# Chunked delta-rule attention on one core: another order of the same work on TensorE, VectorE, ScalarE and GpSimd

## The chip, the cores and the metric

The kernel runs as one program on one core of a Trainium2 chip. The metric is the device time of one execution in microseconds (us). Below, PE is TensorE, PEld its weight loads, DVE is VectorE, ACT is ScalarE, POOL is GpSimd, and SP is the engine whose queue issues the DMAs.

## The reference, cut to what matters

The program is a chain of blocks on x of 2 x 2048 rows by 256: an FFN, the attention, the FFN again, a binary-weight FFN, a state-space convolution, and the binary FFN again. The change lies in the attention alone, a gated delta rule with 16 heads of width 16 and chunks of 64 rows:

```python
q = l2norm((x @ Wq).reshape(Bb, Tt, H, K)) / np.sqrt(K)
k = l2norm((x @ Wk).reshape(Bb, Tt, H, K))
v = (x @ Wv).reshape(Bb, Tt, H, K)
gate = (x @ Wg).reshape(Bb, Tt, H, K)
...
P = jnp.where(strict, jnp.einsum('bhncd,bhnmd->bhncm', k_beta, k) * L, 0.0)
Ainv = jnp.eye(C, dtype=P.dtype) + P
Pk = P
for _ in range(int(np.ceil(np.log2(C))) - 1):
    Pk = Pk @ Pk
    Ainv = Ainv + Pk @ Ainv
v = Ainv @ v
k_cumdecay = Ainv @ (k_beta * jnp.exp(g)[..., None])

def step(S, inp):
    q_i, k_i, v_i, kcd_i, g_i, L_i = inp
    attn = jnp.where(tril, jnp.einsum('bhck,bhmk->bhcm', q_i, k_i) * L_i, 0.0)
    v_new = v_i - kcd_i @ S
    o_i = q_i * jnp.exp(g_i)[..., None] @ S + attn @ v_new
    ...
o = o * jax.lax.rsqrt(jnp.mean(o * o, axis=-1, keepdims=True) + 1e-05) * norm_w
o = o * jax.nn.silu(gate)
return o.reshape(Bb, Tt, D) @ Wo
```

## The kernel before, in words

The attention goes over 32 tiles of 128 rows. It works in blocks of 32 rows, so that a tile has four blocks, done in two halves of the state's recurrence. Each engine has its own instruction stream, in which one loop over 41 slots (`for n in range(-1, SLOTS)`) calls short functions; `at(f, t)` calls `f` for tile `t` where such a tile exists. An engine runs its stream strictly in order, and a `wait_ge` on a semaphore holds all that stands behind it. So the order in which the loops name the functions is the schedule, and nothing else decides it. Different functions of one slot work on different tiles:

- **Tile n.** `norm_x` (DVE, normalizes x), `turn_x` (PE, L1051, transposes it), `keep_xt` (ACT, L1252, copies it out of PSUM), `project_qk` (PE, L1060), `squares` (ACT), `sum_qk` and `guess_qk` (DVE), `root_qk` (POOL, twelve small operations of a reciprocal root), `scale_q` and `scale_k` (DVE, L1424 and L1432), `project_vg` (PE, L1070), `keep_gate` (DVE), and on POOL `spread_decays`, `strengths`, `decayed_k`, `decayed_kb`, `decayed_q`.
- **Tile n-1.** `decays`, `turn_kq`, `turn_kb` and `within` (PE; `within` is L1111, the products inside a block), the ACT copies `keep_kq`, `keep_kb`, `keep_qg`, `exp_decays`, and on DVE `keep_within` (L1442 into delta_PT) and `keep_attn` (L1442 into delta_AT).
- **Two tiles at a time, the substitution.** SP writes delta_PT to memory (L1030, four DMAs of a tile). For a pair m it then waits for both tiles' writes, reads the pair back in another layout into delta_PR (L1012, `pair_in`), waits for the end of the substitution of the pair before it, writes that pair's result out (L1017, `pair_back`), waits for it, and reads it into delta_T as 8 DMAs (L1025, four for each tile). The substitution itself (`solve`, L1468 to L1478) is 60 steps on DVE: 30 in an odd slot and 30 in the slot behind it. It starts with a memset (L1468) that waits for the pair to have landed. Every step waits for the step before it, since each uses its result. Steps 0 to 23 work on 30 to 228 columns, steps 24 to 52 on about 130 to 240, and steps 54 to 59 on 84 or fewer.
- **Tile n-5.** `apply` (PE, L1133) needs delta_T; ACT copies its result with `keep_wt` (L1327) and `keep_ut` (L1319). `spread_vk` (L1312, four copies) fills the operand of the next `apply`.
- **Tile Z = n-6, the recurrence.** For each half: `from_values` (L1146), `from_state` (L1163), ACT `keep_y`, PE `to_state` (L1180), DVE `own_heads` (L1486, into delta_Bm) and `new_state` (L1493, L1498). POOL's `fade_first`, `middle_state`, `fade_second` and ACT's `widen` stand beside it. Then `outputs` (L1195, L1200) and ACT's `keep_o`.
- **Tiles n-7 and n-8, the output.** `sum_o`, `guess_o` (DVE), `root_o` (POOL), `scale_o` (DVE), `gate_o` (POOL, L1637), `turn_o` (PE, L1211), `keep_ot` (ACT, L1371), `project_o` (PE, L1219), `add_o` (DVE, L1516, adds to the residual), `new_stats`.

PSUM bank 7 is shared: its lower half holds the turned o, and one quarter of it the state's product; its upper half holds first the turned x and then the result of `project_o`.

## Time and profile before

| | |
|---|---|
| three runs | 1584.12, 1571.48, 1567.22 us; median 1571.48 |
| profiled execution | 1571.99 us, span 1570.2 us |
| busy, share of the span | PE 77%, DVE 68%, POOL 38%, ACT 32% |
| mean granted TensorE clock | 0.856 of full speed |
| the attention's slots | from about 306 us to 1042 us of the span |

The profile page gives the busy time of each engine and a picture of the span in 40 slices. The attention is the stretch in which DMA traffic is steady at 50 to 57 GB/s, and what runs into it and out of it. Rows below come from three views: the list of waits (which operation stood idle for which other one, summed), the timeline of one engine, and the table of busy time by stretch.

### The profile page before, as it was taken

The page shows a single profiled execution, that of the slowest core. Times are in us where ns is not written, and L with a number is a line of the kernel's source. Part 1 is how long each engine was busy: PE and PEld are TensorE (multiplying, and loading weights), DVE is VectorE, ACT ScalarE, POOL GpSimd, SP SyncE. Part 2 cuts the span into 40 slices and gives each one's busy share as a digit, 9 for nine tenths or more (in the row PEclk, how much of TensorE's full clock was granted, in tenths as well). Part 3 has the DMA queues.
Part 4 walks back from the last instruction along what each step waited for, and adds up shares of the span by engine and source line. Part 5 has one row for each costly group of instructions (what it writes and reads, how often), then busy time and mean ns, then how long its engine had stood idle before and what let it go on. Part 6 is the DMA issues. An engine that isn't in the chain of part 4 may idle for free. (4 is left out here: it accounts for less than half of the span.)

```text
span 1570.2 us, 42564 instructions
## 1 busy us (share of the span) xinstructions
PE 1206.5 (77%) x17194; PEld 893.8 (57%) x17194; DVE 1065.2 (68%) x2897; ACT 500.5 (32%) x1287; POOL 601.3 (38%) x1253
## 2 busy tenths in 40 slices
PE   0888878665788888888888887758889775898938
PEld 0667767432456555565555555647677652466726
DVE  5556654338778778788888777546665677997174
ACT  0221112232555555555555554522211113000001
POOL 1233320154466566566666553323333233200004
PEclk9989995576899899899999987879998897896569
DMA  7000000012222222222222222100000034153102
GB/s 184 0 1 1 1 25 22 7 28 54 50 48 37 49 51 57 57 57 57 56 57 57 57 53 54 30 2 1 1 0 1 26 95 107 49 139 98 37 11 97
DMA packets 192739, 71.21 MB, mean 45 GB/s; under 512 B 139296, under 2 KB 187808, under 8 KB 192544
## 3 DMA queue, kind: packets, MB, share of 16 engines
q1 hardware_dynamic: 190944, 65.87, 18.0%
q8 instruction: 137, 2.24, 0.6%
q10 hardware_dynamic: 1600, 2.62, 0.5%
q14 instruction: 58, 0.48, 0.1%
HBM read 43.03 MB, written 21.23 MB: 41 GB/s over the span
## 5 line engine op out<-in xcount | busy, mean ns | idle before, releaser
L464 POOL TENSOR_TENSOR ffn_H<-ffn_hid,ffn_H 128x512 fp32r<-128x512 f32 x96 | 124.6, 1298 | 267.8 <-DVE ffn_H L439 267.8
L1478 DVE TENSOR_TENSOR delta_PR<-delta_PR,delta_tmp 128x30 f32<-128x30 f32 (+14 forms) x480 | 177.3, 369 | 11.5
L1476 DVE TENSOR_TENSOR delta_tmp<-delta_PR 128x30 f32<-128x30 f32 (+14 forms) x480 | 175.1, 365 | 10.1
L435 DVE TENSOR_TENSOR ffn_hid<-ffn_silu,psum 128x512 f32<-128x512 f32 x96 | 66.1, 688 | 87.4 <-PE psum L368 81.5
L405 ACT ACTIVATE ffn_silu<-psum 128x512 f32<-128x512 f32 x96 | 57.5, 599 | 205.1 <-PE psum L368 205.1
L368 PE MATMUL psum<-ffn_XT,w_gate 128*128 128x512 f32 x384 | 117.7, 432 | 3.9 <-DVE ffn_XT L427 3.9
L1344 ACT ACTIVATE delta_wide<-delta_S 32x128 f32<-32x128 f32 x256 | 78.6, 307 | 113.9 <-POOL delta_S L1623 56.1
L368 PE MATMUL psum<-ffn_XT,w_up 128*128 128x512 f32 x384 | 113.4, 420 | 0.0
L381 PE MATMUL psum<-w_down,ffn_H 128*128 128x256 f32 x768 | 94.2, 282 | 5.3 <-POOL ffn_H L464 5.3
L538 ACT ACTIVATE binary_XT<-psum 128x512 f32<-128x512 f32 x32 | 17.8, 595 | 252.2 <-PE psum L503 252.2
L381 PEld LDWEIGHTS psum<-w_down,ffn_H 128*128 128x128 f32 x768 | 93.5, 188 | 7.4 <-POOL ffn_H L464 6.1
L333 PE MATMUL psum<-consts,ffn_xn 128*128 128x128 f32 x128 | 24.2, 350 | 95.3 <-DVE ffn_xn L305 95.3
L599 POOL TENSOR_TENSOR late_X<-binary_Y,late_X 128x512 f32<-128x512 f32 x16 | 20.8, 1297 | 194.0 <-DVE binary_Y L575 194.0
L1060 PE MATMUL psum<-both_w_in,delta_xT_t 128*128 128x512 f32 x128 | 86.3, 809 | 8.9 <-DVE delta_Kn L1432 7.4
L1133 PE MATMUL psum<-delta_T,delta_pad 128*32 128x128 f32 x2048 | 75.9, 307 | 21.8 <-DMA delta_T<-inverse_scratch 21.7
L368 PEld LDWEIGHTS psum<-ffn_XT,w_up 128*128 128x128 f32 x384 | 79.3, 206 | 19.5
L368 PEld LDWEIGHTS psum<-ffn_XT,w_gate 128*128 128x128 f32 x384 | 78.2, 211 | 21.0 <-DVE ffn_XT L427 4.7
L1732 PEld LDWEIGHTS psum<-space_U,space_T 128*128 128x128 f32 x512 | 78.9, 246 | 19.0 <-issue 19.0
L1732 PE MATMUL psum<-space_U,space_T 128*128 128x32 f32 x512 | 79.0, 327 | 9.2 <-DVE late_X L1806 9.1
L1133 PEld LDWEIGHTS psum<-delta_T,delta_pad 128*32 128x32 f32 x2048 | 65.3, 125 | 25.5 <-DMA delta_T<-inverse_scratch 24.1
L333 PEld LDWEIGHTS psum<-consts,ffn_xn 128*128 128x128 f32 x128 | 18.7, 177 | 102.1 <-DVE ffn_xn L305 55.6
L1146 PE MATMUL psum<-consts,delta_UT 128*32 128x128 f32 x512 | 49.8, 319 | 31.9 <-DVE delta_Bm L1486 30.1
(256 smaller groups left out, 2768.8 us busy)
## 6 DMA issues: line engine op xcount, KB each, us to landing
space_T<-taps_scratch SPq DMA_DIRECT2D x16, 1024.0 KB, 5.6
within_scratch<-delta_PT SPq DMA_DIRECT2D x128, 64.0 KB, 2.0
delta_PR<-within_scratch SPq DMA_DIRECT2D x16, 512.0 KB, 4.4
inverse_scratch<-delta_PR SPq DMA_DIRECT2D x16, 512.0 KB, 5.3
delta_T<-inverse_scratch SPq DMA_DIRECT2D x128, 64.0 KB, 2.4
X<-in_x SPq DMA_DIRECT2D x32, 128.0 KB, 9.8
late_X<-X SPq DMA_DIRECT2D x64, 64.0 KB, 2.0
out<-late_X SPq DMA_DIRECT2D x8, 512.0 KB, 2.9
```

The lines of the kernel that those rows point to most:

```text
L368: i = pe.matmul(bank[:], w[:, k * HID + m * P:k * HID + (m + 1) * P].bitcast(F32R), M.XT[b % 2][hl][k].bitcast(F32R), start=(k == 0 and hl ...
L381: i = pe.matmul(o, M.H[b % 2][hl][:, m * 512 + j * P:m * 512 + (j + 1) * P].bitcast(F32R), B.w_down[:, m * DM:(m + 1) * DM].bitcast(F32R), ...
L405: a.activation(M.silu[n % 3], B.bank[n % 2][:], ACT.Silu, scale=1.0 / 127.0).then_inc(S.silu, 1)
L435: v.tensor_tensor(M.hid[n % 3], M.silu[n % 3], B.bank[2 + n % 2][:], ALU.mult).then_inc(S.hid, 1)
L464: g.tensor_tensor(lo.bitcast(F32R), M.hid[n % 3], hi, ALU.subtract).then_inc(S.hid_lo, 1)
L1060: i = pe.matmul(bank[4][:], M.xT_t[:, k * P:(k + 1) * P], M.w_in[:, k, 0:512], start=(k == 0), stop=(k == 1))
L1133: i = pe.matmul(bank[3][SUB * c:SUB * c + SUB, (2 * w + g) * P:(2 * w + g + 1) * P], M.pad[:, from_c:from_c + SUB], M.T[t % 2][:, h * P:(h ...
L1146: pe.matmul(bank[6][SUB * q:SUB * q + SUB, g * P:(g + 1) * P], M.UT[:, g * P + SUB * q:g * P + SUB * q + SUB], B.ident, start=(g == 0), st ...
L1344: i = a.activation(states(M.wide[half])[rows, :, SUB * c:SUB * c + SUB], states(X)[rows, :, :], ACT.Copy)
L1476: i = v.tensor_tensor(t3, column.to_broadcast([P, j, n_after]), row.to_broadcast([P, j, n_after]), ALU.mult)
L1478: i = v.tensor_tensor(after, after, t3, ALU.add)
L1732: m = pe.matmul(bank[6 + i % 2][:, c * NT:(c + 1) * NT], M.T[i % 4][:, c * P:(c + 1) * P], M.U[:, :, i * CPG + c], start=True, stop=True)
```

## The change

No operation, operand or buffer changes. The order in the four loops does, one condition of a wait is added, and `decayed_kb` now handles tile n and not tile n-1 in slot n.

```diff
--- before.py
+++ after.py
@@ -1047,6 +1047,8 @@
             pe.wait_ge(S.p_xt, t)
         if t > LAG_SCAN:
             pe.wait_ge(S.s_bm, 2 * (t - LAG_SCAN))
+        if t > LAG_OUT:
+            pe.wait_ge(S.o_t, t - LAG_OUT)
         for k in range(KD):
             i = pe.transpose(bank[7][:, DM + k * P:DM + (k + 1) * P], M.xn_t[:, k * P:(k + 1) * P], B.ident)
         i.then_inc(S.p_xt_ps, 1)
@@ -1222,21 +1224,21 @@
     for n in range(-1, SLOTS):
         Z = n - LAG_SCAN
         at(from_values, Z, 0)
-        at(project_qk, n)
+        at(turn_x, n)
         at(project_o, n - LAG_OUT - 1)
         at(from_state, Z, 0)
+        at(project_qk, n)
+        at(to_state, Z, 0)
+        at(decays, n - LAG_FORM)
+        at(project_vg, n)
+        at(turn_kb, n - LAG_FORM)
+        at(from_values, Z, 1)
         at(turn_kq, n - LAG_FORM)
-        at(project_vg, n)
-        at(to_state, Z, 0)
-        at(turn_kb, n - LAG_FORM)
-        at(decays, n - LAG_FORM)
-        at(from_values, Z, 1)
         at(from_state, Z, 1)
         at(apply, n - LAG_APPLY)
         at(to_state, Z, 1)
         at(outputs, Z)
         at(within, n - LAG_FORM)
-        at(turn_x, n + 1)
         at(turn_o, n - LAG_OUT)
 
 
@@ -1373,22 +1375,22 @@
     for n in range(-1, SLOTS):
         Z = n - LAG_SCAN
         at(widen, Z, 0)
+        at(keep_y, Z, 0)
         at(squares, n)
-        at(keep_y, Z, 0)
+        at(exp_decays, n - LAG_FORM)
+        at(widen, Z, 1)
+        at(tanh_g, n)
         at(keep_v, n)
-        at(tanh_g, n)
         at(keep_kq, n - LAG_FORM)
+        at(keep_kb, n - LAG_FORM)
+        at(keep_y, Z, 1)
         at(keep_qg, n - LAG_FORM)
-        at(widen, Z, 1)
-        at(keep_y, Z, 1)
-        at(exp_decays, n - LAG_FORM)
         at(keep_wt, n - LAG_APPLY)
-        at(spread_vk, n - LAG_PAD)
-        at(keep_kb, n - LAG_FORM)
         at(keep_ut, n - LAG_APPLY)
+        at(keep_ot, n - LAG_OUT)
         at(keep_xt, n + 1)
         at(keep_o, Z)
-        at(keep_ot, n - LAG_OUT)
+        at(spread_vk, n - LAG_PAD)
 
 
 def delta_vector(v, own, B, M, S, run):
@@ -1521,38 +1523,32 @@
 
     for n in range(-1, SLOTS):
         Z, O = n - LAG_SCAN, n - LAG_OUT
+        at(add_o, O - 1)
         at(guess_o, O)
-        at(add_o, O - 1)
-        solve(n, 0, 2)
+        at(norm_x, n + 1)
+        at(own_heads, Z, 0)
         at(sum_qk, n)
-        solve(n, 2, 7)
-        at(own_heads, Z, 0)
-        solve(n, 7, 8)
         at(new_state, Z, 0)
-        solve(n, 8, 9)
         at(guess_qk, n)
-        solve(n, 9, 14)
+        solve(n, 0, 11)
         at(keep_gate, n)
-        solve(n, 14, 16)
+        solve(n, 11, 17)
         at(scale_o, O)
-        solve(n, 16, 18)
+        solve(n, 17, 22)
         at(own_heads, Z, 1)
-        solve(n, 18, 19)
-        at(norm_x, n + 1)
-        solve(n, 19, 22)
+        solve(n, 22, 24)
+        at(keep_within, n - LAG_FORM)
+        solve(n, 24, 25)
         at(scale_q, n)
-        solve(n, 22, 23)
+        solve(n, 25, 26)
+        at(new_state, Z, 1)
+        solve(n, 26, 27)
         at(scale_k, n)
-        at(keep_within, n - LAG_FORM)
-        solve(n, 23, 24)
+        solve(n, 27, 28)
+        at(sum_o, O + 1)
+        solve(n, 28, 30)
+        at(keep_attn, n - LAG_FORM)
         at(new_stats, O - 1)
-        solve(n, 24, 26)
-        at(sum_o, O + 1)
-        solve(n, 26, 28)
-        at(new_state, Z, 1)
-        solve(n, 28, 29)
-        at(keep_attn, n - LAG_FORM)
-        solve(n, 29, 30)
 
 
 def delta_gpsimd(g, own, B, M, S, run):
@@ -1639,16 +1635,16 @@
     for n in range(-1, SLOTS):
         Z, O = n - LAG_SCAN, n - LAG_OUT
         at(fade_first, Z)
+        at(middle_state, Z)
         at(root_o, O)
-        at(middle_state, Z)
         at(root_qk, n)
         at(fade_second, Z)
         at(gate_o, O)
+        at(decayed_q, n)
+        at(strengths, n)
+        at(decayed_k, n)
+        at(decayed_kb, n)
         at(spread_decays, n)
-        at(decayed_k, n)
-        at(decayed_kb, n - 1)
-        at(strengths, n)
-        at(decayed_q, n)
 
 
 
```

Three places, by the instruction order of a slot boundary in the middle of the stage. In these rows L-numbers of the changed kernel are 2 higher on PE, ACT and DVE. First **DVE at the start of an odd slot, before**; the rows begin with `new_state` of the slot that ends:

```order
L1478 TENSOR_TENSOR delta_PR<-delta_PR,delta_tmp 128x29x2
L1498 TENSOR_TENSOR delta_S<-delta_E,delta_Bm 128x128
L1476 TENSOR_TENSOR delta_tmp<-delta_PR 128x30
L1442 TENSOR_TENSOR delta_AT<-psum,delta_E 128x256 x2
L1478 TENSOR_TENSOR delta_PR<-delta_PR,delta_tmp 128x30
L73 TENSOR_SCALAR delta_o_work<-delta_o_ss 128x16
L74 TENSOR_SCALAR delta_o_work<-delta_o_work 128x16
L1507 TENSOR_SCALAR delta_o_work<-delta_o_work 128x16
L1516 TENSOR_TENSOR X<-psum,X 128x256
L1468 MEMSET delta_PR 128x32
L1476 TENSOR_TENSOR delta_tmp<-delta_PR 128x30
```

**The same place now**, from `add_o` to the memset that begins a pair's substitution:

```order
L1518 TENSOR_TENSOR X<-psum,X 128x256
L73 TENSOR_SCALAR delta_o_work<-delta_o_ss 128x16
L74 TENSOR_SCALAR delta_o_work<-delta_o_work 128x16
L1509 TENSOR_SCALAR delta_o_work<-delta_o_work 128x16
L305 TENSOR_SCALAR delta_xn_t<-X,ln_mean_var,ln_rstd 128x256
L1488 TENSOR_TENSOR delta_Bm<-psum,consts 128x128
L1408 TENSOR_REDUCE delta_ssq<-delta_sq 128x32
L1495 TENSOR_TENSOR delta_X<-delta_E,delta_Bm 128x128
L73 TENSOR_SCALAR delta_rs_work<-delta_ssq 128x32
L74 TENSOR_SCALAR delta_rs_work<-delta_rs_work 128x32
L1413 TENSOR_SCALAR delta_rs_work<-delta_rs_work 128x32
L1470 MEMSET delta_PR 128x32
```

The memset stood directly behind `guess_o` and `add_o`. It now stands behind `norm_x`, both operations of the state's first half, and the sum and guess for q and k as well, and eleven steps follow it in one run.

**PE around the start of a slot, before**, from `within` of the slot that ends to `from_state`:

```order
L1111 MATMUL psum<-delta_MV,delta_KbT 32x128 x32
L1051 MATMUL psum<-consts,delta_xn_t 128x128 x2
L1211 MATMUL psum<-consts,delta_o_sb 128x128 x2
L1146 MATMUL psum<-consts,delta_UT 32x128 x4
L1060 MATMUL psum<-both_w_in,delta_xT_t 128x512 x2
L1219 MATMUL psum<-both_w_out,delta_oT 128x256 x2
L1163 MATMUL psum<-delta_S,delta_WT 32x32 x16
```

**and now**, to the first `to_state`:

```order
L1113 MATMUL psum<-delta_MV,delta_KbT 32x128 x32
L1213 MATMUL psum<-consts,delta_o_sb 128x128 x2
L1148 MATMUL psum<-consts,delta_UT 32x128 x4
L1053 MATMUL psum<-consts,delta_xn_t 128x128 x2
L1221 MATMUL psum<-both_w_out,delta_oT 128x256 x2
L1165 MATMUL psum<-delta_S,delta_WT 32x32 x16
L1062 MATMUL psum<-both_w_in,delta_xT_t 128x512 x2
L1182 MATMUL psum<-delta_y_block,delta_Kd 32x32 x16
```

The transpose of x stood in front of the transpose of o and of `from_values`, a slot ahead of its use. It now stands behind both and directly in front of `project_o`, and `project_qk` has moved behind `from_state`.

**ACT around the start of a slot, before**, from `keep_wt` to `widen`:

```order
L1327 ACTIVATE delta_WT<-psum,consts 128x256 x4
L1312 ACTIVATE delta_pad<-delta_VK 128x8x16 x4
L1292 ACTIVATE delta_KbT<-psum 128x256
L1319 ACTIVATE delta_UT<-psum 128x256
L1252 ACTIVATE delta_xT_t<-psum 128x256
L1362 ACTIVATE delta_o_sq<-psum 128x256
L1365 ACTIVATE delta_o_sb<-psum 128x256
L1371 ACTIVATE delta_oT<-psum 128x256
L1344 ACTIVATE delta_wide<-delta_S 32x4x32 x4
```

**and now**, to `keep_y`:

```order
L1329 ACTIVATE delta_WT<-psum,consts 128x256 x4
L1321 ACTIVATE delta_UT<-psum 128x256
L1373 ACTIVATE delta_oT<-psum 128x256
L1254 ACTIVATE delta_xT_t<-psum 128x256
L1364 ACTIVATE delta_o_sq<-psum 128x256
L1367 ACTIVATE delta_o_sb<-psum 128x256
L1314 ACTIVATE delta_pad<-delta_VK 128x8x16 x4
L1346 ACTIVATE delta_wide<-delta_S 32x4x32 x4
L1357 ACTIVATE delta_y_block<-psum 32x256 x2
```

`keep_ut` now follows `keep_wt` directly, the copy of o comes ahead of that of x, and the four copies of `spread_vk` have moved behind `keep_o`.

## Rows read from the trace of the kernel before

**Rows 1.** Waits on DVE, 503 to 872 us: line waited for, us in total, times, longest
```profile
DVE delta_PR L1468 <- DMA delta_PR<-within_scratch: 27.5, 9, 3.5
DVE delta_PT L1442 <- PE psum L1111: 14.3, 12, 3.7
```

**Rows 2.** The same view of PE's waits, same stretch
```profile
PE psum L1146 <- DVE delta_Bm L1486: 13.6, 14, 2.3
...
PE psum L1111 <- ACT delta_UT L1319: 11.0, 12, 1.5
PE psum L1133 <- DMA delta_T<-inverse_scratch: 8.1, 9, 1.4
```

**Rows 3.** DVE in order of time: start us, us, engine, line, op, out<-in, count, idle before
```profile
503.19 0.76 DVE L1442 TENSOR_TENSOR delta_PT<-psum,delta_E 128x256 f32<-128x256 f32 x2 [0.79 <-PE psum L1111]
...
709.89 0.76 DVE L1442 TENSOR_TENSOR delta_PT<-psum,delta_E 128x256 f32<-128x256 f32 x2
...
718.67 0.09 DVE L1468 MEMSET delta_PR<- 128x32 f32 x1 [3.33 <-DMA delta_PR<-within_scratch]
...
731.61 0.76 DVE L1442 TENSOR_TENSOR delta_PT<-psum,delta_E 128x256 f32<-128x256 f32 x2
...
750.46 0.76 DVE L1442 TENSOR_TENSOR delta_PT<-psum,delta_E 128x256 f32<-128x256 f32 x2
...
872.12 0.76 DVE L1442 TENSOR_TENSOR delta_PT<-psum,delta_E 128x256 f32<-128x256 f32 x2 [0.47 <-PE psum L1111]
```

**Rows 4.** The DMA queue of SP in order of time, behind the first part of 709.89
```profile
710.67 1.93 SPq L1030 DMA_DIRECT2D within_scratch<-delta_PT  x4
...
714.55 0.43 SPq L1017 DMA_DIRECT2D inverse_scratch<-delta_PR  x1
719.84 0.32 SPq L1025 DMA_DIRECT2D delta_T<-inverse_scratch  x1
```

**Rows 5.** PE in order of time, the long slot from 709.78 on
```profile
709.78 0.44 PE L1051 MATMUL psum<-consts,delta_xn_t 128*128 128x128 f32 x2
...
721.43 0.64 PE L1146 MATMUL psum<-consts,delta_UT 128*32 128x128 f32 x8 [2.29 <-DVE delta_Bm L1486]
...
723.68 3.12 PE L1133 MATMUL psum<-delta_T,delta_pad 128*32 128x128 f32 x64 [0.62 <-DMA delta_T<-inverse_scratch]
...
730.03 1.54 PE L1111 MATMUL psum<-delta_MV,delta_KbT 32*32 32x128 f32 x64 [1.21 <-ACT delta_UT L1319]
```

**Rows 6.** PE in order of time, the short slot from 731.50 on
```profile
743.67 1.91 PE L1133 MATMUL psum<-delta_T,delta_pad 128*32 128x128 f32 x61
...
748.25 0.64 PE L1200 MATMUL psum<-delta_y_block,delta_AT 128*32 128x16 f32 x52 [0.88 <-issue]
749.37 1.06 PE L1111 MATMUL psum<-delta_MV,delta_KbT 32*32 32x128 f32 x64 [0.48 <-ACT delta_UT L1319]
```

**Rows 7.** Busy time in a stretch: PE, PEld, DVE, ACT, POOL with counts, PEclk, DMA share, GB/s
```profile
724.00:727.00 3.00, 3.00 (x96) 2.66 (x88) 2.40 (x8) 0.87 (x3) 2.26 (x9) 0.65 0.33 49
```

**Rows 8.** ACT in order of time: the copy of the turned x
```profile
710.52 0.38 ACT L1252 ACTIVATE delta_xT_t<-psum 128x256 f32<-128x256 f32 x1 [1.98 <-PE psum L1051]
```

**Rows 9.** DVE in order of time: two steps of the substitution and an independent operation
```profile
659.60 0.40 DVE L1478 TENSOR_TENSOR delta_PR<-delta_PR,delta_tmp 128x234 f32<-128x234 f32 x1
660.03 0.40 DVE L1476 TENSOR_TENSOR delta_tmp<-delta_PR 128x228 f32<-128x228 f32 x1
660.35 0.28 DVE L1486 TENSOR_TENSOR delta_Bm<-psum,consts 128x128 f32<-128x128 f32 x1
```

**Rows 10.** POOL in order of time: first operation of root_o and gate_o, short slot
```profile
738.19 0.21 POOL L86 TENSOR_TENSOR delta_o_work<-delta_o_work 128x16 f32<-128x16 f32 x1 [1.31 <-DVE delta_o_work L1507]
...
749.23 0.78 POOL L1637 TENSOR_TENSOR delta_o_sb<-delta_o_sb,delta_gate 128x256 f32<-128x256 f32 x1
```

**Rows 11.** The last slots: POOL's last root_o, and DVE's add_o, in order of time
```profile
1033.57 0.21 POOL L86 TENSOR_TENSOR delta_o_work<-delta_o_work 128x16 f32<-128x16 f32 x1 [4.89 <-DVE delta_o_work L1507]
...
1033.99 0.42 DVE L1516 TENSOR_TENSOR X<-psum,X 128x256 f32<-128x256 f32 x1 [0.50 <-PE psum L1219]
```

## The prediction

> **What bounds the kernel now.** I first read the waits of DVE. Its largest is the memset that opens a pair's substitution: 27.5 us over nine pairs, 3.06 each [rows 1]. Taken alone this promises much, since the change puts that memset behind other work. So I read the order of time, to see whether the memset's wait ends last. I take the start of `keep_within` (delta_PT) as the mark of a slot. From 503.19 to 872.12 us there are 18 slots, 368.9 us: 41.0 us a pair [rows 3]. The two slots of a pair differ. From 709.89 to 731.61 is 21.7 us, the **long** slot, with the memset and its wait of 3.33 us; from 731.61 to 750.46 is 18.85 us, the **short** one, and in it DVE waits for nothing [rows 3]. The reader is to see two different limits there.
>
> The short slot is bound by DVE's own work. The long slot is bound by a chain through memory. `keep_within` starts at 709.89, SP issues the write of delta_PT at 710.67, the solved pair's write at 714.55 (together with the read of the new pair), the reads of delta_T at 719.84 [rows 4], and `apply` starts at 723.68 on their landing [rows 5]. That is 13.8 us from `keep_within`. In this slot PE had lost 2.29 us on `own_heads` and then waits another 0.62 for delta_T [rows 5]. The waits of PE say the same of all nine pairs: 8.1 us for delta_T, nine times [rows 2]. So wherever PE was made late by DVE, it was still early for the DMA. The 13.6 us that PE waits for delta_Bm [rows 2] lie ahead of the DMA's landing, and most of them can't be had.
>
> **The change, part by part.** The sum is made against the profiled execution, 1572.0 us; the median of the three runs, 1571.5, is the same for this purpose.
>
> *The memset goes behind the state's update.* From `keep_within` to the memset there were 8.8 us, 3.3 of them wait [rows 3]. Nine operations move into that stretch: `scale_q`, `scale_k`, `norm_x`, `own_heads`, `sum_qk`, `new_state` and the three of `guess_qk`. At 0.3 us each (between the 0.28 and 0.40 of [rows 9], less the overlap there) they fill 2.7 us, and the wait falls to about 0.5. DVE has 2.6 us more room in each long slot. On the path this is worth 0: the chain of DMAs hangs on `keep_within` and on the transfers, of which none is moved. Its last condition, the end of the substitution before it, is met when the write is issued, since in the changed order it lies no more than two short operations of 0.3 us further from `keep_within`, and `keep_attn` and `new_stats` go behind it. What is late next is delta_T: PE now waits for it about 3 us in one piece, and not 0.6 behind 2.3. If that cover were gone, 2.6 us a pair would come free.
>
> *`keep_ut` directly behind `keep_wt`.* `within` waited for `keep_ut` 1.21 us in the long slot [rows 5] and 0.48 in the short one [rows 6], 11.0 us in 12 slots [rows 2]. Between `apply` and `keep_ut` stood five ACT copies that have moved. Behind `apply`, the long slot is path to its end, so this counts: of 1.2 us a pair (11.0 by 9) I take 0.9, since the short slot's part is hidden by DVE and part of the rest becomes waiting for instructions, as the 0.88 before the second piece of L1200 shows [rows 6]. Bounds: 0.3 and 1.2.
>
> *The substitution in longer runs.* 30 steps stood in 15 pieces in a slot and stand in 9. So six more steps follow the step whose result they need. Such a step starts 0.43 us behind its predecessor's start (659.60 to 660.03), while an independent operation starts after 0.32 (660.03 to 660.35), before the one ahead has ended [rows 9]. That is 0.11 us, 0.66 in a slot. In the long slot the room above hides it. In the short slot it is path: 18.85 becomes 19.5. Against it stands that `keep_within` waits 14.3 us for `within` in 12 of 18 slots [rows 1], 0.8 us a slot; in short slots PE comes earlier than DVE now, so I let 0.5 us of it go. Net 0.15 us a pair; bounds 0 and 0.66. Here the Trainium skill says otherwise: in "VectorE: DVE Perf Modes", section "The DRAIN you can't avoid", the next operation waits for the pipe to empty in any case and a semaphore between two of them costs nothing. By it this term would be 0 or, with the wait that goes, a gain. The row shows the overlap; the same page leaves room for it in its last sentence on operations that are not held.
>
> *x turned in the slot that needs it.* On PE there is now a ring of handovers at the slot's start: `turn_o`, its copy, `turn_x`, its copy, `project_o`. `from_values` covers the first copy. Nothing covers the second: from the start of the transpose at 709.78 [rows 5] to the end of its copy at 710.90 [rows 8] are 1.1 us, of which the transpose itself needs 0.3, so 0.8 to 0.9 us of PE are lost in each slot with the hop to `project_o`. Behind PE in that time stand `from_state`, `to_state` and with them `own_heads`. In the long slot the wait for delta_T hides it. In the short slot PE would need 18.85 - 0.48 + 0.9 = 19.3 us at most, against DVE's 19.5: hidden, barely. The new wait on the copy of o is met by the same ring. Priced at 0; with no cover, 1.8 us a pair.
>
> *The clock.* `apply` ran 3.12 us in the long slot, at a granted clock of 0.65 of full speed (1.2 GHz for part of it, 2.4 for the rest) [rows 5, 7], and 1.91 us in the short one [rows 6]. What PE did before was to wait, 2.3 and 0.6 us. With one wait of 3 us this will be more frequent: I take 0.2 us a pair, bounds 0 and 1.2.
>
> *Both ends.* In the first slots the memset waits too and the chain is the same; I take 2 us of gain in all, between 0 and 6, which is none or two pairs' memset waits of 3.06. At the end `add_o` now stands before `guess_o`: POOL's last `root_o` began at 1033.57, and can now begin only when `add_o` (1033.99, 0.42 us) and three small operations are through, about 1.4 us later, once [rows 11].
>
> Sum: a pair changes by -0.9 + 0.15 + 0.2 = -0.55 us. Of 16 pairs 14 run under full load, so -7.7; with -2 and +1.4 it is -8. I forecast **1563.5 us** (1572.0 - 8), own range 1555 to 1571.
>
> **The rivals.** *A: the DMA is not the limit.* If delta_T lands 2 us or more earlier, because fewer DMAs and copies meet, the long slot loses the memset's wait as well: -2.6 more in a pair, reduced by the 0.5 or so by which DVE is then next. 14 x 2.1 = 29 us below my forecast, 1535; half of it, 1549, if every second pair does so. For it speak the size of the two waits on DVE [rows 1, 2]; against it the nine waits for delta_T. Chance 0.2.
>
> *B: slower, by a ring through POOL.* `root_o` now stands behind `middle_state`, which waits for `own_heads`. From `root_o`'s first operation at 738.19 to the end of `gate_o` at 750.01 POOL needs 11.8 us in the short slot [rows 10]. `gate_o` releases `turn_o`; from there to `own_heads` PE and ACT need about 6.5 with the gap above (of the 9.4 us from 709.78 to 719.14 [rows 5], where PE's wait begins, I estimate 5.6 to be in the ring: the rest belongs to `project_vg`, `decays` and the transposes of k and q). Together 18.3, under DVE's 19.5. It decides as soon as it exceeds that: if PE's part runs at the low clock (3.12 by 1.91, 1.6 times), 3.4 us more, 21.7. Then every short slot takes 2.2 us more: 14 x 2.2 = 31, 1594. Chance 0.12.
>
> *C: no effect.* The clock drops behind every wait for delta_T. Then `apply` costs its 3.12 us in each long slot, 1.0 more than I have: 14 us, 1577. The Trainium skill has this as a rule ("TensorE: Matmul & The Clock Gate", section "HAM oscillation — how this bites in real kernels": waits for DMAs put the array back to half its clock, each time). The rows show it once in two slots. Chance 0.16.
>
> *D: the run costs nothing*, the skill's rule above: the short slot stays at 18.85 or less, 14 x 0.66 = 9 us less, 1554. Chance 0.08.
>
> **How the numbers follow.** My forecast has 0.44. About 1%, 15.7 us, is what a measurement of this kernel tells from no change. Faster by more than that (under 1556) are A, most of D and a tail of my own case: 0.2 + 0.06 + 0.04 = 0.3. Slower (over 1587) are B and a tail of C: 0.13. Between them 0.57. The range takes in half of A, D and C and leaves out B and the full A: 1541 to 1584.
>
> **What would show it.** In the changed profile the memset's wait should be under 1 us a pair, and that of `apply` for delta_T 2.5 us or more, with 13.8 us from `keep_within` to `apply` as before. PE's wait for `keep_ut` should be gone. A new idle time of 0.5 to 0.9 us should stand before `project_o`, released by ACT's copy of x. DVE should have no wait in the short slot, and that slot should be 19.3 to 19.6 us, the long one 21 us. I am wrong if the distance from `keep_within` to `apply` shrinks (A), if `turn_o` waits for `gate_o` (B), or if short slots get no longer (D).

## The result: 2.4% slower, and the profile after

The changed kernel takes 1612.2 us (median of 4 runs, 1605.8 to 1615.9) against 1570.6 for the kernel before in the same session (4 runs, 1567.2 to 1584.1). The ratio is 1.024, 95% interval 1.017 to 1.032. Forecast were 1563.5 us and a range up to 1584: wrong, and on the side to which I gave 0.13.

The profiled execution has a span of 1607.0 us, 36.8 more than before. The attention, from the first transpose of x to the last `add_o`, takes 767.6 us where it took 735.7: 31.9 of it. The middle 18 slots, from `keep_within` to `keep_within`, take 391.93 us and took 368.93 [rows 3]. Two rows say what the engines did in these stretches, first of the kernel before, then of the changed one. Columns: the stretch, its length, busy us and count of PE, PEld, DVE, ACT, POOL, then PEclk, the DMA share, GB/s.

```profile
503.19:872.12 368.93, 309.74 (x7975) 214.47 (x7976) 306.15 (x981) 205.44 (x594) 229.76 (x613) 0.94 0.26 55
```

```profile
505.18:897.11 391.93, 327.35 (x7976) 222.97 (x7976) 317.35 (x982) 208.05 (x594) 229.73 (x612) 0.90 0.25 51
```

The same matmuls keep PE busy 17.6 us longer, at a granted clock of 0.90 of full speed in place of 0.94, and PE is idle 5.4 us longer. DVE's idle time grows too. So which engine waits for which? The waits of PE in the changed kernel, same stretch (line waited for: us in total, times, longest), answer to [rows 2]:

```profile
PE psum L1113 <- issue: 19.3, 11, 2.4
PE psum L1135 <- DMA delta_T<-inverse_scratch: 14.7, 6, 4.1
PE psum L1202 <- issue: 14.0, 15, 1.8
PE psum L1221 <- ACT delta_xT_t L1254: 10.2, 18, 0.6
```

In the kernel before two rows of this view, which I had not given a term of their own, were:

```profile
PE psum L1200 <- issue: 13.5, 13, 2.1
...
PE psum L1111 <- issue: 8.0, 8, 2.4
```

And the waits of DVE after, which answer to [rows 1]:

```profile
DVE delta_PT L1444 <- PE psum L1113: 31.1, 14, 4.0
DVE delta_Bm L1488 <- PE psum L1182: 19.5, 14, 2.5
DVE delta_PR L1470 <- DMA delta_PR<-within_scratch: 4.2, 5, 2.4
```

The reader is to see a turn of roles. The memset's wait fell from 27.5 to 4.2 us and PE's waits for delta_Bm (13.6) and `keep_ut` (11.0) are gone: what the change does to these waits it does. But DVE now waits 50.6 us for PE in its two largest rows, and PE waits for DVE hardly at all. PE sets the pace in both slots of a pair. What it then waits for most, 33.3 us, stands under "issue": the profile shows nothing that holds it. Here is one such stall, PE in order of time in the long slot that starts at 808.28 (start us, us, engine, line, op, out<-in, count, idle before):

```profile
807.82 0.41 PE L1113 MATMUL psum<-delta_MV,delta_KbT 32*32 32x128 f32 x5 [1.93 <-issue]
...
808.53 0.72 PE L1148 MATMUL psum<-consts,delta_UT 128*32 128x128 f32 x8
...
810.44 2.05 PE L1221 MATMUL psum<-both_w_out,delta_oT 128*128 128x256 f32 x4 [0.56 <-ACT delta_xT_t L1254]
...
824.37 1.95 PE L1135 MATMUL psum<-delta_T,delta_pad 128*32 128x128 f32 x64 [1.55 <-DMA delta_T<-inverse_scratch]
826.26 0.38 PE L1182 MATMUL psum<-delta_y_block,delta_Kd 32*32 32x32 f32 x32
826.57 0.67 PE L1197 MATMUL psum<-delta_wide,delta_QgT 128*32 128x128 f32 x16
827.03 1.25 PE L1202 MATMUL psum<-delta_y_block,delta_AT 128*32 128x16 f32 x120
830.01 0.26 PE L1202 MATMUL psum<-delta_y_block,delta_AT 128*32 128x16 f32 x8 [1.73 <-issue]
830.35 1.06 PE L1113 MATMUL psum<-delta_MV,delta_KbT 32*32 32x128 f32 x64
```

`outputs` stops after 120 of its 128 small matmuls, for 1.73 us, and goes on with the last 8. They read and write what the 120 did; no semaphore stands between them. DVE and the others are done by 828.5 and stand too. So PE lacked its next instructions. What brings them is in the DMA part of the profile, as a queue of kind "instruction". In the stretch 826.6 to 828.2 it reads (queue, kind: packets, MB, share of the engines):

```profile
q8 instruction: 1, 0.02, 3.9%
```

That packet starts at 827.6, and between 828.2 and 830.0, in most of which all engines stand, no packet at all moves. Over the 18 slots q8 carries 63 packets in both kernels, for 15,952 matmuls and weight loads: 253 of them to a packet, beside PE's own waits, which are instructions too. PE's stalls under issue of over 0.3 us all end 2.1 to 3.0 us behind the start of such a packet, and no two packets start less than 3.3 us apart, in either kernel.

One more count settles what these stalls are. Number all of PE's records in order of time, matmuls, weight loads and waits. In the kernel before, the first record behind each stall of over 0.3 us under issue (22 in the 18 slots) then stands an exact multiple of 256 behind the first of them, and the last one 15,360 records and 60 packets behind it. In the changed kernel it is the same for its 23, within 3 records. So PE stops only where one packet's 256 instructions end and the next packet's begin.

### The profile page after: what moved, and what is told of

Same layout as the page of the kernel before. It is cut to its first block, busy times and chain, and to the rows that moved or that the text cites. A ratio compares the mean times of both kernels' runs of the same rounds, so it can differ in the third digit from the quotient of the medians.

```text
span 1607.0 us, 42559 instructions
## 1 busy us (share of the span) xinstructions
PE 1233.6 (77%) x17194; PEld 907.1 (56%) x17194; DVE 1088.4 (68%) x2897; ACT 504.9 (31%) x1287; POOL 604.8 (38%) x1253
## 4 chain that ended last, share of the span: by engine, by line
PE 26%; DVE 14%; DMA 5%; issue 5%; SPq 2%; POOL 1%; ACT 0%; POOLq 0%; DVEq 0%; ACTq 0%
PE psum L368 6%; PE psum L381 3%; PE psum L1728 3%; PE psum L519 3%; DMA inverse_scratch<-delta_PR 2%; PE psum L1135 2%; DMA within_scratch<-delta_PT 1%; DVE ln_stats L293 1%; SPq L613 1%; DMA delta_T<-inverse_scratch 1%; PE psum L1202 1%; DVE ffn_xn L305 1%; PE psum L503 1%; DVE delta_tmp L1478 1%; PE psum L333 1%
## 5 line engine op out<-in xcount | busy, mean ns | idle before, releaser
L1480 DVE TENSOR_TENSOR delta_PR<-delta_PR,delta_tmp 128x30 f32<-128x30 f32 (+14 forms) x480 | 173.8, 362 | 12.5
L1062 PE MATMUL psum<-both_w_in,delta_xT_t 128*128 128x512 f32 x128 | 82.2, 775 | 20.8 <-DVE delta_Kn L1434 20.2
L333 PEld LDWEIGHTS psum<-consts,ffn_xn 128*128 128x128 f32 x128 | 20.4, 190 | 101.8 <-DVE ffn_xn L305 55.6
L1600 POOL TENSOR_TENSOR delta_Qg<-delta_Qn,both_eg 128x256 f32<-128x256 f32 x32 | 22.8, 712 | 135.9 <-DVE delta_Qn L1426 135.9
```

Source lines behind the costliest of these rows:

```text
L333: i = pe.transpose(B.bank[4 + k][:, j * P:(j + 1) * P], xn[:, j * DM + k * P:j * DM + (k + 1) * P], B.ident)
L1062: i = pe.matmul(bank[4][:], M.xT_t[:, k * P:(k + 1) * P], M.w_in[:, k, 0:512], start=(k == 0), stop=(k == 1))
L1480: i = v.tensor_tensor(after, after, t3, ALU.add)
```

## The experiments

All are timed against the kernel before on the same chip; the pairs' lengths come from one profiled execution each. The edits that only move a step show the loop's lines.

**First, parts undone or done alone.** My theory then was the uncovered handover of x (step *x turned in the slot that needs it*), and the rival that DVE's longer runs cost.

```diff
 # e1: the changed kernel's delta_tensor, and no wait for o_t
-        at(turn_x, n)
...
+        at(turn_x, n + 1)
         at(turn_o, n - LAG_OUT)
```

> The changed kernel with one thing undone: PE turns x at the end of the slot before, in front of the transpose of o, and the wait on the copy of o goes. All other orders stay new. Theory T (handovers at the slot's start make PE the bound): the 0.56 us that project_o waits for the copy of x goes in 18 of 18 slots of the middle stretch, and with the hops around it 0.8 to 0.9 us a slot; 31 slots give 25 us or more, and the granted clock recovers from 0.90 towards 0.94, so 1612 falls to 1575-1588. Rival R (the runs of the substitution on DVE): under 8 us, 1604 or more. Rival M (PE is slow because its waits for instructions and the clock are worse, whatever the order at the slot's start): 1600 or more, with the waits of within for instructions still near 19 us in 18 slots.

Measured 1613.1 us, ratio 1.019 (1.014 to 1.024). The gap before `project_o` shrinks to 2.4 us in all, and nothing clear of the noise is won (1.019 against 1.024): PE now waits for delta_T and for its instructions, as rival M had it.

```profile
PE psum L1133 <- DMA delta_T<-inverse_scratch: 34.1, 9, 5.6
PE psum L1111 <- issue: 16.8, 10, 2.2
PE psum L1200 <- issue: 13.6, 12, 1.9
```

The theory fell as the main cause.

```diff
 # e2: delta_tensor's loop as before, the other three changed
 # e3: delta_vector's loop as before, the other three changed
```

> The changed kernel with the whole of PE's order as before; DVE, ACT and POOL new. Theory T: as with x alone turned back, 1575-1588, and the rest of PE's order makes under 6 us. If the rest of PE's order (project_qk behind from_state, decays ahead of project_vg) is what costs, this is faster than turning x back alone by over 10 us. Rival R: 1604 or more.

Measured 1650.4 us, ratio 1.042 (1.037 to 1.047).

> The changed kernel with DVE's order as before; PE, ACT and POOL new. Theory T: DVE's order is not the cause and has given PE some slack, so this is no faster than the changed kernel, 1610-1635, since the memset's wait of 3 us a pair returns on top of PE's gap. Rival R: it takes back the loss, 1585 or less.

Measured 1648.3 us, ratio 1.042 (1.037 to 1.047). Each engine's new order needs the others': with PE's old one DVE waits 44.5 us for delta_Bm, with DVE's old one 31.5 us at the memset. So the parts don't add up, and neither run prices DVE's runs.

```diff
 # e4: the kernel before, with the wait for o_t, and keep_ot ahead of keep_xt on ACT
         at(from_values, Z, 0)
+        at(turn_x, n)
...
-        at(turn_x, n + 1)
```

> The kernel before with x turned in the slot that needs it (PE), the wait on the copy of o, and on ACT the copy of o ahead of that of x, which this needs; nothing else. Theory T: PE has 0.8 us less in each of 31 slots; in short slots DVE hides at most half of it, so 1571 becomes 1585-1600. Rival R or M: within 6 us of 1571.

Measured 1605.0 us, ratio 1.016 (1.010 to 1.022). Put into the old order alone the step costs 25 us by the ratio, which is in theory T's range of 14 to 29 us. But again it shows in more than its gap:

```profile
PE psum L1202 <- issue: 15.6, 15, 2.0
PE psum L1113 <- issue: 15.6, 10, 2.8
PE psum L1062 <- ACT delta_xT_t L1254: 8.5, 18, 0.5
```

Idle time under issue is 31.2 us against 21.5 before. The middle 18 slots take 30.4 us more than before, and PE is idle for only 3.2 of them: the same matmuls keep it busy 27.2 us longer, at a granted clock of 0.86 in place of 0.94. So the range was met, and the mechanism, 0.8 us less of PE in each slot, was not. This made the instructions the suspect. The row of e4's 18 slots:

```profile
508.83:908.15 399.32, 336.95 (x7975) 222.25 (x7976) 304.20 (x982) 206.61 (x594) 223.94 (x614) 0.86 0.24 50
```

**Second, the packets and the write of delta_PT.** In some long slots the read of the new pair is issued 5.2 us after the write's first DMA, in others 3.5. The waits of SP's queue show it, first from 720.8 to 726 us, then from 762.8 to 769, both of the changed kernel:

```profile
SPq L1010 <- DMA within_scratch<-delta_PT: 1.5, 1, 1.5
```

```profile
SPq L1010 <- DMA within_scratch<-delta_PT: 3.2, 1, 3.2
```

In the second slot a 16 KB packet of PE's starts at 765.6, amid the write's 2112 packets; in the first one it starts at 724.7, behind them. I call a landing late when that read is issued more than 4.25 us after the write's first DMA. Late landings stand in 7 of the 14 last long slots after, 1 of 14 before, 10 of 14 in the run with x turned at the end. The next runs add matmuls ahead of the attention, only to shift the packets against the slots. (My expectations give packet times 0.7 us too late: I had read them against another origin. By the profile's origin the harmful ones of the changed kernel start 1.2 to 3.3 us after the write's first issue; three others, at 3.2 to 3.3 us, did no harm.)

All sixteen traces of this document together have 256 such reads, and they show the packets to be the cause. With a packet of PE's that starts 0.8 to 2.9 us after the write's first issue 61 of 61 landings are late, by 0.8 to 2.1 us. With none in the first 3.6 us 149 of 161 reads are issued within 4.0 us, and the latest at 4.33. Between 2.9 and 3.6 us, at the write's end, 11 of 31 are late.

```diff
 # gates_tensor, ahead of the wait for a_decay; e5 and e6: 112, e7: 32
+    for _ in range(112):
+        pe.matmul(bank[2][0:32, 0:128], B.unseen_r, B.ident_r, start=True, stop=True)
```

> The changed kernel with 112 small matmuls more on PE ahead of the attention, beside a wait of 9.6 us, so that PE's 16 KB instruction packets fall at other places of the slots; nothing else differs. Theory F (the packets): in the changed kernel's trace the write of delta_PT ends 1.2 to 1.7 us late in the long slots in which a packet starts 2 to 3.7 us after the write's first issue, 6 of the 15 long slots. Shifted, 0 to 2 of them do: 5 to 8 us less than the changed kernel, ratio to the kernel before 1.017 to 1.021. Rival N (late landings are covered, or come from something else): as many late landings, or the same time, ratio 1.022 to 1.027.

Measured 1600.4 us, ratio 1.017 (1.012 to 1.022), with late landings in 7 of 14 slots, as many as unshifted. The time is in theory F's range, but its condition, two late landings at most, was not met, so it decides nothing.

> The changed kernel with turn_x back at the end of the slot (as measured: 1613.1, ratio 1.019, 10 of 12 long slots with a late landing) and with the same 112 matmuls more ahead of the attention. Theory F: 2 or fewer late landings, 12 to 16 us less, ratio 1.009 to 1.012. Rival N: ratio 1.017 to 1.021.

Measured 1592.3 us, ratio 1.011 (1.007 to 1.015), late landings in 7 of 14 in place of 10. In its trace a pair with a late landing takes 44.2 us, one without 42.2. The direction is theory F's, but its condition, 2 late landings or fewer, was not met here either; 3 landings fewer explain 6 us of the 13, and the intervals of the two runs touch.

> The kernel before with 32 small matmuls more on PE ahead of the attention, so that packets that started 4.2 to 5.2 us after the write's first issue (no late landing there, 1 of 12 long slots had one) start earlier, inside the write. Theory F: late landings in half of the long slots or more, 8 to 20 us more, ratio 1.005 to 1.013. Rival N: 1 to 3 us more, for the matmuls added, ratio 1.000 to 1.002.

Measured 1574.3 us, ratio 1.000 (0.998 to 1.003), late landings in 1 of 14. The shift did not bring the packets where I wanted them, so it tells nothing against either theory.

**Third, one step of the prediction.**

```diff
 # e8: the kernel before, delta_scalar
         at(keep_wt, n - LAG_APPLY)
+        at(keep_ut, n - LAG_APPLY)
         at(spread_vk, n - LAG_PAD)
         at(keep_kb, n - LAG_FORM)
-        at(keep_ut, n - LAG_APPLY)
```

> The kernel before with one step moved on ACT: keep_ut directly behind keep_wt, ahead of spread_vk and keep_kb. By the prediction's step on keep_ut PE's wait for delta_UT in the long slots goes, 0.9 us a pair: 13 us less, ratio 0.991. Rival: the slots' length is set by DVE and by the T chain, and PE's wait is only moved: ratio 0.998 to 1.002. Rival 2: keep_kb and spread_vk, now 0.7 us later, hold PE's within or DVE: slower, ratio 1.003 to 1.01.

Measured 1572.2 us, ratio 0.999 (0.997 to 1.002). The wait for `keep_ut` is gone, and another stands in its place:

```profile
PE psum L1111 <- issue: 9.4, 10, 2.0
PE psum L1111 <- ACT delta_KbT L1292: 9.1, 13, 1.2
```

**Fourth, gap, clock and instructions.**

```diff
 # e9: the changed kernel, delta_tensor
         at(turn_x, n)
+        at(from_state, Z, 0)
         at(project_o, n - LAG_OUT - 1)
-        at(from_state, Z, 0)
```

> The changed kernel with one step moved on PE: from_state(Z, 0), 32 small matmuls, between turn_x and project_o, so that PE has work while ACT copies x^T. Theory G (the gap of 0.56 us before project_o in nearly every slot is paid in full, because PE sets the slot): the gap goes, 8 to 18 us less than the changed kernel, ratio to the kernel before 1.008 to 1.016 against 1.017 to 1.024 for the changed kernel. Rival H (the idle time only moves to PE's next stall): same ratio as the changed kernel, the time is found again under issue before L1202 and L1113.

Measured 1604.3 us, ratio 1.021 (1.016 to 1.027): rival H by the time, though not by the place. The idle time before `project_o` is gone in all 18 slots. It is found again not under issue (27.4 us before L1202 and L1113 in place of 33.3) but before `apply`, where the wait for delta_T is 29.4 us in place of 14.7, and `from_state` waits 11.2 us for delta_S.

```diff
 # e12: the changed kernel, apply, ahead of the wait for delta_T, where f is even
+                for _ in range(3):
+                    pe.matmul(bank[3][:], B.ident_r, B.unseen_r.unsqueeze(1).to_broadcast([P, NH, SUB]), start=True, stop=True)
```

> The changed kernel with 3 matmuls of 512 columns more ahead of apply in every second slot (those in which apply waits for T), into a bank that apply then overwrites: PE works while it waits. They take 1.3 to 2.4 us where the wait is 0 to 4.7 us. Theory K (the lower granted clock behind the idle times, 75 us at the lower level against 48 before, is a loss that more work in the wait gives back): granted clock up by 0.02 or more in the middle of the attention, time not above the changed kernel's, ratio 1.010 to 1.022. Rival L (the clock isn't won back, and the added matmuls are paid where the wait is shorter than they are): 5 to 15 us more, ratio 1.025 to 1.034.

Measured 1607.9 us, ratio 1.023 (1.018 to 1.029), and the clock did not rise:

```profile
505.96:903.86 397.90, 340.64 (x8002) 229.56 (x8003) 316.74 (x982) 208.02 (x594) 229.78 (x612) 0.89 0.25 51
```

Theory K is not borne out, and the time is in rival L's range no more than the clock is in K's. The filler cost nothing either, since it stands in the wait for delta_T, which fell to 11.8 us.

```diff
 # e10: the changed kernel, e11: the kernel before; outputs
-        for h in range(NH):
+        for h in range(0, NH, 2):
             for q in range(4):
                 i = pe.matmul(bank[5][...], M.AT[...], M.yq[...], start=False, stop=(h == NH - 2), ...)
```

The profile records each of these f32 matmuls twice, so 32 calls fewer are 64 records.

> The changed kernel with part of the computation left out: outputs adds the product of every second head only, 64 small matmuls fewer a slot (128 PE instructions). Theory I (PE is stopped by the supply of its instructions in the dense end of the slot: 51 us of idle under issue between 330 and 985, each 1.6 to 2.0 us long and ending about 2 us after the start of a 16 KB packet): not only the 0.6 us of matmuls a slot goes but most of these stalls: 40 to 60 us less, ratio 0.985 to 1.000. Rival J (only the matmuls' own time): 15 to 22 us less, ratio 1.003 to 1.014.

Measured 1558.6 us, ratio 0.991 (0.988 to 0.994).

> The kernel before with the same 64 small matmuls a slot left out. Theory I: 36 us of idle under issue between 330 and 985 mostly goes, but DVE and the T chain then set the slot, 10 to 30 us less, ratio 0.981 to 0.994, and the distance between the two orders shrinks to under 1.5%. Rival J: ratio 0.990 to 1.000 and the distance stays at 1.7 to 2.4%.

Measured 1554.9 us, ratio 0.989 (0.984 to 0.994). The two orders now differ by 0.2%. From the changed kernel 3.3% went (1.024 to 0.991, on two chips; e9 and e12, near copies of the changed kernel, stood at 1.021 and 1.023 on the second), from the kernel before 1.1%. PE's waits in e10, the first by what holds it and then those under issue:

```profile
PE psum L1113 <- ACT delta_UT L1321: 8.9, 14, 0.7
...
PE psum L1113 <- issue: 3.9, 9, 1.0
PE psum L1202 <- issue: 1.5, 3, 0.8
```

33.3 us under issue became 5.4, with 55 packets in place of 63. The granted clock of the 18 slots is back at 0.93. But PE's own time had gone as well, 0.53 us a slot: in slots without a stall the 128 small matmuls take 1.31 us and the 64 take 0.78. The last two runs give that time back in few instructions.

```diff
 # e13: e10's kernel, e14: e11's kernel; within, behind its waits
+        for r in range(2):
+            pe.matmul(bank[r][:, 0:DM], B.ident_r, B.unseen_r.unsqueeze(1).to_broadcast([P, 8, SUB]), start=True, stop=True)
```

> The changed kernel with every second head left out of outputs' last product (as measured: ratio 0.991 to the kernel before) and with two matmuls of 256 columns added ahead of within, whose output within overwrites: 0.64 us of TensorE work by the 0.64 us from start to start of a 512 column one, about what was taken away, but in 4 instructions where 128 went. Theory I (supply of instructions): the stalls under issue stay gone, at most 0.4 us a slot comes back: ratio 0.991 to 1.001. Rival J (it was the engine's time): the time that went comes back, ratio 1.010 or more.

Measured 1567.6 us, ratio 0.996 (0.993 to 0.999).

> The kernel before with the same part left out (measured: ratio 0.989) and the same two wide matmuls added. Theory I: within comes up to 0.64 us later where it isn't held by delta_UT, ratio 0.989 to 0.999, and no more than 0.7% from the changed order with the same edit. Rival J: ratio 0.999 to 1.003 and the changed order 1.5 to 2.4% behind it.

Measured 1567.6 us, ratio 0.995 (0.992 to 0.998). Both kernels take the same time. One slot's end of e13, in order of time:

```profile
600.78 0.50 PE L1111 MATMUL psum<-unseen_r,ident_r 128*128 128x256 f32 x2
601.22 1.07 PE L1115 MATMUL psum<-delta_MV,delta_KbT 32*32 32x128 f32 x64
```

From start to start the two added matmuls take 0.44 us, less than the 0.64 that I had reckoned. So about 0.1 us a slot of the 0.53 was not given back, 3 us in 32 slots, 0.2%. The changed order came down by 2.8% all the same. PE's stalls under issue:

```profile
PE psum L1204 <- issue: 3.3, 6, 0.9
PE psum L1115 <- issue: 0.5, 2, 0.3
```

Theory I holds for the changed order: it is the supply of instructions, not the engine's time. The clock goes with it, 0.93 in the 18 slots of e13 against 0.90 in the changed kernel:

```profile
502.28:867.87 365.59, 313.62 (x6860) 213.08 (x6858) 315.50 (x982) 208.03 (x594) 228.33 (x612) 0.93 0.27 55
```

In the old order the stalls go too (2.6 us in e14), and only 0.5% is won. What stands in their place is the wait for `keep_ut`, in e14's view of PE's waits:

```profile
PE psum L1109 <- ACT delta_UT L1321: 30.4, 18, 2.1
```

That is 18 slots of 18, where the kernel before had 11.0 us in 12 [rows 2]. In e14 the filler ahead of `within` starts 2.5 to 2.9 us after the first of the 64 small matmuls, as `within` does after the first of 128 in 14 of 18 slots of the kernel before: in that order `keep_ut` sets the time, and a stall of up to 1 us is hidden in front of it. The changed order has removed that wait, so there each stall is paid. Once they are gone PE waits for other things in e13, 18.6 us for delta_T, 10.2 for the copy of x and 7.8 for `gate_o` (0.7 in the changed kernel), and the two orders end at the same time.

Of late landings e13 has 8 in 14 long slots and e14 has 2, and the times are still equal: they cost (a pair with one takes 42.1 us in e13, without 39.7), but they are not what makes the change slower by 2.4%.

## Why the prediction was wrong

The step that failed first is the bound: PE was held to be off the path except where a semaphore stops it. The gain for `keep_ut`, the price of 0 for x and the fixed 13.8 us of the chain all rest on it, in part or whole.

**The bound: failed.** I had DVE's work as the limit of the short slot and the chain through memory as that of the long one, and asked of PE only which semaphore it waited for. The 21.5 us under issue beside those waits I used once, for "part of the rest becomes waiting for instructions". In the kernel before, PE's waits for `keep_ut` and delta_Bm, 24.6 us, cost little, for the next packet could come meanwhile. So the order in which the loops name the functions is not all that decides the schedule, as I wrote of the kernel before: when PE's next packet comes does too. The changed order closes them, puts `from_state`, `apply`, `to_state`, `outputs` and `within` more tightly in a row, and 33.3 us of issue stand where 32.5 of issue and `keep_ut` stood. What the order gave PE, its instructions took. A pair of the middle takes 2.6 us more where I had it 0.55 us less: of the 23.0 us of nine pairs 5.4 are idle time of PE, and for 17.6 it is busy longer with the same matmuls, at the lower granted clock.

**`keep_ut`, -0.9 a pair: failed.** This is the step that carried the forecast's sign. Its wait is gone as forecast, but e8 shows it worth 0 alone (0.999, 0.997 to 1.002): what stands behind it is `keep_kb`, and the packets.

**x turned in its slot, priced at 0: failed.** Its place and size were right (0.56 us in each of 18 slots). Its cover was not. In the long slot I let it hide in the wait for delta_T, in the short one behind DVE at 19.5 us, "barely". With PE's stalls of up to 1.9 us there PE is behind DVE, and nothing covers the gap. Alone it costs 1.6% (e4), which is near my uncovered price of 1.8 us a pair (25 us in 14 pairs), but in part by luck: most of it showed as a lower clock. Filling it in the changed kernel (e9) wins nothing measurable, since PE then waits for delta_T or its packets. So it is a cause beside the supply, and not an addend.

**The chain's 13.8 us: failed.** I held the transfers fixed, because none is moved. From `keep_within` to `apply` the nine long slots take 13.5 to 16.4 us after, 15.0 on average, against 13.4 to 14.8 and 14.1 before. The transfers aren't moved, but PE's packets are, against them. The four slots of the nine whose write lands late are the four over 15 us. A pair with a late landing takes 44.2 us in the changed kernel, one without 43.2. Rival A would have shortened this distance; it grew.

**The memset: right.** 27.5 us became 4.2, under 1 a pair, and as forecast none of it was won.

**The short slot: right in one of nine.** The slot from 742.76 takes 19.33 us, forecast 19.3 to 19.6, and its one stall under issue is 0.60 us. The nine take 20.4 on average. The runs' price of 0.15 a pair isn't tested by that, since DVE is no longer the limit, and stays open, and rival D with it. DVE's busy time did rise by 11.2 us, 0.62 a slot, near the 0.66 of six more steps; that fits the size and doesn't show what it costs.

**The clock, +0.2 a pair: too small.** PE's same work takes 17.6 us more in nine pairs, up to 2 us a pair; my bound was 1.2. Most drops come behind stalls for instructions: of the 13 stretches at the lower of the clock's two levels (1.2 GHz) that begin in the 18 slots, 8 begin 1.1 to 2.4 us behind the end of a stall of 1.4 to 1.9 us under issue, and in e13, where no such stall is left, the granted clock is 0.93 again. The stall before 807.82 is one of the 8: the granted clock is 0.50 from 810 to 814 us. Rival C had the clock drop behind waits for delta_T. In this slot it stays at 1.00 with such a wait in it, from 822 to 824 us.

```profile
810.00:812.00 2.00, 1.56 (x4) 1.18 (x4) 1.93 (x7) 1.99 (x9) 1.31 (x3) 0.50 0.75 120
812.00:814.00 2.00, 2.00 (x34) 1.58 (x32) 1.93 (x7) 0.74 (x3) 2.00 (x4) 0.50 0.14 22
...
822.00:824.00 2.00, 0.83 (x30) 0.71 (x26) 1.90 (x6) 1.96 (x5) 1.51 (x7) 1.00 0.43 64
```

**Both ends, -2 and +1.4: failed.** Outside the middle 18 slots the attention lost 8.9 us (31.9 - 23.0). That the limit is the same there I take to be so; no run shows it. (The sum itself, -7.7 - 2 + 1.4, is -8.3 and gives 1563.7 us, not 1563.5, which decides nothing.)

**Rival B**, slower by a ring through POOL, had the sign and not the mechanism: `turn_o` waits 0.7 us once for `gate_o` in 18 slots. With fewer instructions the ring does come close: the wait is 9.1 us in 10 slots of e10.

What stays open: how the loss divides between the stalls, the clock that falls behind them and the gap of x. No run separates them: e9 filled the gap and e12 the wait, and both only moved idle time, while e10 and e13 took stalls and low clock away together. Nor do stalls alone lower the clock: e14 has 2.6 us of them and a granted clock of 0.90, and 12 of its 18 stretches at the lower level begin within 2.2 us of the end of a wait of 1.6 to 2.1 us for `keep_ut`. The 7.7 us lost after the attention (535.8 us against 528.1), where no instruction differs, are not to be put down to the change: in the sixteen traces this stretch takes 528.1 to 536.3 us, and the longest is e11's, which has the order of before.

## What to carry to other kernels

Idle time under issue is a resource like any other: before an order is closed up, add it to the waits that the change removes, and where it is large in a run of small matmuls, take a removed wait as worth nothing until the instructions are fewer. Whether such idle time is a lack of instructions can be read from one trace: number the engine's records and see whether the stalls stand a multiple of 256 apart. A handover's gap is hidden only while the engine that has it isn't the bound, so price it once with the cover and once without. Transfers that aren't moved may still land later, when the moved engine's instruction packets fall into them.

## What the runs showed of the hardware

PE can be stopped amid a group of small matmuls by the supply of its instructions. In the middle 18 slots of the sixteen traces it stood 277 times for over 0.3 us under issue, and all but 3 of these stalls (in e2) stand at a multiple of 256 records, within 3. Their length was up to 2.4 us in the two main kernels, behind 3.3 us with 239 to 430 records, where 3.3 us is the least distance of two packets. Not each such stretch ends in a stall: all slots of e13 have one of 327 to 356 records in 3.3 us, and 6 stalls of over 0.3 us came of it. How far ahead PE is supplied stays open. The Trainium skill, "Runtime: NRT & Kernel Launch", section "Instruction fetch mechanics", has the blocks of 16 KB and 256 instructions, and the trace agrees to the record. It also calls this fetching hidden, because the sequencer issues more slowly than the blocks arrive. The traces here disagree: 33.3 us of 391.9 were such stalls in the changed kernel, 5.4 with an eighth fewer packets.

A 16 KB packet of PE's, which takes 0.9 to 1.5 us in the changed kernel, delays the landing of a write in 2112 small packets that it falls into by 0.8 to 2.1 us, in 61 of 61 cases.
